# Local attention reads the token-shifted x in place, its tile loop written out

## What is computed

```python
def shift_token(t):                      # second half of the channels from the token before
    t1, t2 = jnp.split(t, 2, axis=-1)
    t2 = jnp.pad(t2, ((0, 0), (1, 0), (0, 0)))[:, :-1]
    return jnp.concatenate([t1, t2], axis=-1)

h = shift_token(x)
q, k, v = jnp.split(h @ wqkv, 3, axis=-1)       # 8 heads of 64
q, k = rotary_xpos(l2norm(q) * qs, l2norm(k) * ksc)
x = x + local_attention(q, k, v) @ wo           # windows of 64, each sees itself and the one before
h = layer_norm(shift_token(x)) * lg + lb
a, g = jnp.split(h @ w1 + b1, 2, axis=-1)
x = x + (a * gelu(g)) @ w2 + b2
```

## Time and profile before

| | us |
|---|---|
| median of 3 runs (1795.16 to 1800.93) | 1795.65 |
| the profiled execution | 1793.86 |
| its span, first to last instruction | 1792.0 |
| first local attention, projection to last add_y | 1199.9 to 1426.7 |
| second | 1489.0 to 1716.4 |
| PE busy | 1565.2 (87%) |
| DVE busy | 1209.4 (67%) |
| ACT busy | 1096.4 (61%) |
| POOL busy | 533.5 (30%) |

### The profile page before, as it was taken

One profiled execution on the slowest core, in us unless ns is written; L12 is line 12 of the kernel. 1 busy time (PEld: TensorE's weight loads), 2 busy tenths in 40 slices (PEclk: granted clock), 3 DMA queues, 4 the chain that ended last, 5 costly groups with the idle time before them and its releaser, 6 DMA issues. The chain is left out here.

```text
span 1792.0 us, 31754 instructions
## 1 busy us (share of the span) xinstructions
PE 1565.2 (87%) x10386; PEld 1060.9 (59%) x10386; DVE 1209.4 (67%) x2313; ACT 1096.4 (61%) x2369; POOL 533.5 (30%) x479
## 2 busy tenths in 40 slices
PE   6999999999769999999888888858888786898875
PEld 4777777777548888888632323325555553656543
DVE  2676676676457777777666766747878646788744
ACT  2555555555258888888546666636776634767641
POOL 1222222232122222222100000027666504666621
PEclk9999999999669999999878988988999998999988
DMA  7000000000012122221000000000000000000000
GB/s 218 1 2 1 0 0 0 0 0 1 0 50 71 70 70 71 75 75 60 0 0 1 1 0 1 1 1 1 1 1 0 0 1 1 1 2 0 0 0 24
DMA packets 18812, 36.05 MB, mean 20 GB/s; under 512 B 5606, under 2 KB 10850, under 8 KB 16546
## 3 DMA queue, kind: packets, MB, share of 16 engines
q1 hardware_dynamic: 18738, 35.08, 5.8%
HBM read 33.90 MB, written 1.18 MB: 20 GB/s over the span
## 5 line engine op out<-in xcount | busy, mean ns | idle before, releaser
L873 DVE TENSOR_TENSOR m_hidp<-m_hid,m_hidp 128x512 fp32r<-128x512 f32 x260 | 182.1, 725 | 81.8 <-ACT m_hidp L832 81.6
L389 ACT ACTIVATE a_prob<-ps,a_negmax 128x512 f32<-128x512 f32 (+3 forms) x256 | 133.8, 525 | 143.8 <-DVE a_negmax L460 143.8
L837 ACT ACTIVATE m_hid<-ps,pre_w 128x512 f32<-128x512 f32 x260 | 176.9, 685 | 51.5 <-PE ps L937 51.4
L937 PE MATMUL ps<-m_xp,m_w1p 128*128 128x512 f32 x780 | 191.9, 396 | 8.1 <-DVE m_xp L865 7.2
L967 PE MATMUL ps<-m_hidp,m_w2p 128*128 128x512 f32 x768 | 189.1, 394 | 0.0
L1140 ACT ACTIVATE c_sb_pT<-ps 128x1024 f32<-128x1024 f32 x128 | 130.3, 1024 | 89.9 <-PE ps L1321 88.6
L1605 ACT ACTIVATE l_sb_prob<-ps,l_sb_negmax,l_sb_rn 128x192 f32<-128x192 f32 (+1 forms) x256 | 123.9, 494 | 92.1 <-DVE l_sb_negmax L1702 92.0
L344 POOL TENSOR_TENSOR a_qk_r<-a_qk_c,a_qk_s 128x512 f32<-128x512 f32 x64 | 81.5, 1273 | 331.0 <-DVE a_qk_s L451 331.0
L1198 DVE TENSOR_REDUCE c_sb_negmax<-ps 128x2 f32<-128x1024 f32 x128 | 153.8, 1220 | 38.7 <-PE ps L1305 38.2
L937 PEld LDWEIGHTS ps<-m_xp,m_w1p 128*128 128x128 f32 x780 | 148.8, 191 | 41.5 <-DVE m_xp L865 7.3
L967 PEld LDWEIGHTS ps<-m_hidp,m_w2p 128*128 128x128 f32 x768 | 144.1, 188 | 33.7
(11 more groups left out here) (227 smaller groups left out, 3360.9 us busy)
## 6 DMA issues: line engine op xcount, KB each, us to landing
m_gate_all<-m_gates_d SPq DMA_DIRECT2D x16, 1024.0 KB, 4.6
pre_w<-w1T SPq DMA_DIRECT2D x14, 258.0 KB, 2.7
pre_w<-w2T SPq DMA_DIRECT2D x14, 256.0 KB, 2.8
pre_wqkv<-wqkv SPq DMA_DIRECT2D x2, 768.0 KB
...
```

The costliest lines, as they stand in the source:

```text
L389: nc.scalar.activation(prob[:, u % 4, 0:width(p)], score_ps(b, p, j)[:, 0:width(p)], ACT.Exp, bias=negmax[:, u:u + 1], accum_out=den[:, b ...
L837: nc.scalar.activation(hid[:, c % 2, f, :], ps[:, f, :], ACT.Gelu, bias=w1[:, k, FF + f:FF + f + 1]).then_inc(gelu_done, 1)
L873: nc.vector.tensor_tensor(hidp[:, c % 2, 1, f, :], hid[:, c % 2, f, :], hidp[:, c % 2, 0, f, :], ALU.subtract).then_inc(low_done, 1)
L937: ins = nc.tensor.matmul(ps[:, f, :], w1p[:, k, a, f * P:(f + 1) * P], xp[:, b, c, :], start=(i == 0), stop=(i == 2))
```

## The change

The turned x is stored shifted. The new `shift_halves` writes channels 0 to 63 into columns 0 to 511 of `xT_full` and channels 64 to 127 into columns 1 to 512, in two ACT copies of 64x512. `Norm` does so at the end of `attention1` (new argument `shifted`), and `gated_mlp` in place of L1971; the phases before keep the plain xT. The tile's columns are then both halves' operand in place: `shifted` on PE is only a slice. `hT`, its semaphore and its 72 copies go. DVE zeroes column 0 of the upper 64 partitions, which POOL did for all 128. `each_tile` writes out all 16 steps, and the steps leave out what would touch a tile past 15. `spread` waits for add_y of the tile before, which it had through project_v. The diff, cut to its core:

```diff
+def shift_halves(nc, keep, src, b, done):
+    full = keep["xT_full"]
+    nc.scalar.activation(full[0:64, b, 0:S], src[0:64, :], ACT.Copy)
+    nc.scalar.activation(full[64:P, b, 1:S + 1], src[64:P, :], ACT.Copy).then_inc(done, 1)
...
 class Norm:
...
     def scalar(self, act):
         for b in range(NB):
             act.wait_ge(self.turn_mm, b + 1)
-            self.nc.scalar.activation(self.keep["xT"][:, b, :], self.ps[:, self.banks[b], :],
-                                      ACT.Copy).then_inc(self.turn_ev, 1)
+            if self.shifted:
+                shift_halves(self.nc, self.keep, self.ps[:, self.banks[b], :], b, self.turn_ev)
+            else:
+                self.nc.scalar.activation(self.keep["xT"][:, b, :], self.ps[:, self.banks[b], :],
+                                          ACT.Copy).then_inc(self.turn_ev, 1)
...
-    norm = Norm(nc, ctx, keep, ps, [0, 1, 2, 3], x_add, [QUADS * (b + 1) for b in range(NB)], "cn_")
+    norm = Norm(nc, ctx, keep, ps, [0, 1, 2, 3], x_add, [QUADS * (b + 1) for b in range(NB)], "cn_", shifted=True)
...
     def each_tile(eng, step):
-        for t in range(TPB):
-            step(t, t)
-        with eng.Fori(1, NB) as b:
-            for t in range(TPB):
-                step(TPB * b + t, t)
+        for n in range(NT):
+            step(n, n % TPB)
...
-        nc.gpsimd.memset(keep["xT_pad"], 0.0).then_inc(inited, 1)
...
     @block.vector
     def _(dve):
-        def shifted(n, t):
-            b = n // TPB % NB
-            wait_past(dve, v_mm, n)
-            full = keep["xT_full"]
-            nc.vector.tensor_copy(hT[0:64, :], full[0:64, bass.ds(b, 1), bass.ds(t * P + 1, P)]
-                                  .rearrange("p a n -> p (a n)")).then_inc(hT_done, 1)
-            nc.vector.tensor_copy(hT[64:P, :], full[64:P, bass.ds(b, 1), bass.ds(t * P, P)]
-                                  .rearrange("p a n -> p (a n)")).then_inc(hT_done, 1)
+        nc.vector.memset(xs[64:P, :, 0:1], 0.0).then_inc(inited, 1)
         dve.wait_ge(inited, 4)
-        shifted(0, 0)
...
-        shifted(1, 1)
...
         def step(n, t):
-            shifted(n + 2, (t + 2) % TPB)
             rowmax(n, t, 0)
             rowmax(n, t, 1)
-            squares(n + 1)
+            if n + 1 < NT:
+                squares(n + 1)
...
     @block.tensor
     def _(pe):
+        def shifted(n, t):
+            return xs[:, n // TPB, t * P:(t + 1) * P]
-        def project_qk(n):
-            pe.wait_ge(hT_done, 2 * (n + 1))
+        def project_qk(n, t):
...
-                ins = nc.tensor.matmul(ps[:, w, :], hT[:, :], wqkv[:, w, :], start=True, stop=True)
+                ins = nc.tensor.matmul(ps[:, w, :], shifted(n, t), wqkv[:, w, :], start=True, stop=True)
...
         def spread(n):
             pe.wait_ge(r_wide, n + 1)
-            pe.wait_ge(v_ev, n + 3)
+            pe.wait_ge(v_ev, min(n + 3, NT))
+            wait_past(pe, y_add, n)
...
-            project_qk(n + 2)
+            if n + 2 < NT:
+                project_qk(n + 2, (t + 2) % TPB)
...
             act.wait_ge(x2_mm, b + 1)
-            nc.scalar.activation(xT[:, b, :], ps[:, 7, :], ACT.Copy).then_inc(x2_ev, 1)
+            shift_halves(nc, keep, ps[:, 7, :], b, x2_ev)
```

More of the change, by code:

```diff
@@ L108, in __init__ @@
                 load(self.m_w2[i][0:r, k, :], io["l_w2"][i, k * P:k * P + r, :])
+def shift_halves(nc, keep, src, b, done):
+    full = keep["xT_full"]
+    nc.scalar.activation(full[0:64, b, 0:S], src[0:64, :], ACT.Copy)
+    nc.scalar.activation(full[64:P, b, 1:S + 1], src[64:P, :], ACT.Copy).then_inc(done, 1)
 class Norm:
[L115 removed]
+    def __init__(self, nc, ctx, keep, ps, banks, ready, counts, prefix, shifted=False):
         def sb(name, shape):
@@ L1498, in each_tile @@
     def each_tile(eng, step):
-        for t in range(TPB):
-            step(t, t)
-        with eng.Fori(1, NB) as b:
-            for t in range(TPB):
-                step(TPB * b + t, t)
-    def first(n):
-        return isinstance(n, int) and n == 0
+        for n in range(NT):
+            step(n, n % TPB)
     @block.gpsimd
@@ L1632, in step @@
             exps(n, t, 1)
-            if not first(n):
+            if n:
                 copy_o(n - 1)
             copy_pT(n, t, 1)
-            copy_qk(n + 2)
+            if n + 2 < NT:
+                copy_qk(n + 2)
             exps(n, t, 2)
             exps(n, t, 3)
-            copy_qT(n + 1, (t + 1) % TPB)
+            if n + 1 < NT:
+                copy_qT(n + 1, (t + 1) % TPB)
             copy_pT(n, t, 3)
-            copy_kT(n + 1, (t + 1) % TPB)
-            squares(n + 2)
-            copy_v(n + 2, (t + 2) % TPB)
+            if n + 1 < NT:
+                copy_kT(n + 1, (t + 1) % TPB)
+            if n + 2 < NT:
+                squares(n + 2)
+            if n + 2 < NT:
+                copy_v(n + 2, (t + 2) % TPB)
         each_tile(act, step)
@@ L1722, in add_y @@
             dve.wait_ge(y_mm, n + 1)
-            xt = x[:, bass.ds(n, 1), :].rearrange("p a d -> p (a d)")
-            nc.vector.tensor_tensor(xt, m_ps[:, 0:D], xt, ALU.add).then_inc(y_add, 1)
-        shifted(1, 1)
+            nc.vector.tensor_tensor(x[:, n, :], m_ps[:, 0:D], x[:, n, :], ALU.add).then_inc(y_add, 1)
         rope_c(0, 0)
@@ L1732, in step @@
         def step(n, t):
-            shifted(n + 2, (t + 2) % TPB)
             rowmax(n, t, 0)
             rowmax(n, t, 1)
-            squares(n + 1)
+            if n + 1 < NT:
+                squares(n + 1)
             copy_pT(n, t, 0)
-            rope_sum(n + 1)
+            if n + 1 < NT:
+                rope_sum(n + 1)
             rowmax(n, t, 2)
             rowmax(n, t, 3)
-            if not first(n):
+            if n:
                 normalise(n - 1)
@@ L1744, in step @@
             reciprocal(n, t)
-            rope_c(n + 2, (t + 2) % TPB)
-            if not first(n):
+            if n + 2 < NT:
+                rope_c(n + 2, (t + 2) % TPB)
+            if n:
                 add_y(n - 1)
@@ L1761, in project_qk, with project_v @@
             for w in range(2):
-                ins = nc.tensor.matmul(ps[:, w, :], hT[:, :], wqkv[:, w, :], start=True, stop=True)
+                ins = nc.tensor.matmul(ps[:, w, :], shifted(n, t), wqkv[:, w, :], start=True, stop=True)
             ins.then_inc(qk_mm, 1)
-        def project_v(n):
-            pe.wait_ge(hT_done, 2 * (n + 1))
+        def project_v(n, t):
             wait_past(pe, y_add, n - 2)
             wait_past(pe, v_ev, n)
-            nc.tensor.matmul(m_ps, hT[:, :], wqkv[:, 2, :], start=True, stop=True).then_inc(v_mm, 1)
+            nc.tensor.matmul(m_ps, shifted(n, t), wqkv[:, 2, :], start=True, stop=True).then_inc(v_mm, 1)
         def turn_qk(n, w):
-            pe.wait_ge(raw_done, n + 2)
+            pe.wait_ge(raw_done, min(n + 2, NT))
             pe.wait_ge(qk_norm if w else rope_add, n + 1)
@@ L1840, in output @@
             ins.then_inc(y_mm, 1)
-        project_qk(0)
-        project_v(0)
-        project_qk(1)
-        project_v(1)
+        project_qk(0, 0)
+        project_v(0, 0)
+        project_qk(1, 1)
+        project_v(1, 1)
         turn_qk(0, 0)
@@ L1858, in step @@
             values(n, t, 0)
-            if not first(n):
+            if n:
                 spread(n - 1)
-            turn_qk(n + 1, 0)
+            if n + 1 < NT:
+                turn_qk(n + 1, 0)
             turn_p(n, t, 2)
-            turn_qk(n + 1, 1)
+            if n + 1 < NT:
+                turn_qk(n + 1, 1)
             turn_p(n, t, 3)
-            if not first(n):
+            if n:
                 output(n - 1)
-            project_v(n + 2)
+            if n + 2 < NT:
+                project_v(n + 2, (t + 2) % TPB)
         each_tile(pe, step)
```

13 lines of the change are left out of this document (5 added, 8 removed).

## The result

The changed kernel takes 1775.0 us (median of 4 runs, 1774.23 to 1779.49) against 1796.09 for the kernel before on the same chip (4 runs, 1795.16 to 1800.93): a ratio of 0.9877, 95% interval 0.9848 to 0.9906. The forecast was 1773.0, with a range from 1764 to 1786. The profiled execution took 1775.55 us, its span 1773.7.

What follows compares the result with a forecast made beforehand. A loop of waits across engines, none full, was taken to pace local attention. Gains of 22.7 (steps) and 3.65 (starts) less 4.7 (added copies) gave 21.65 us: 1772.2 from 1793.86, 1774.0 from 1795.65; forecast 1773, range 1764 to 1786.

Steps and rivals of the forecast that it cites:

- Written-out steps: Local attention, steps the loop had rolled: gains of 0.35 us (t = 2, 3), 0.75 (t = 0), 0.8 (t = 1) each.
- the 0.16 just named: Steps with t = 2, 3: part of hT's 0.71 us left at rope_sum, counted inside the 0.35, not added.
- the cover by project_qk: Steps with t = 2, 3: project_qk on PE holds the first transposes, leaving 0.16 of hT's 0.71 us.
- Step 1: Local attention's n = 1, already written out before the change: claimed to gain 0.5 us.
- Last two steps: n = 14, 15: without work on nonexistent tiles 16 and 17 (spare tiles), 4.6 us a layer gained; bounds 2.0 and 6.5.
- Starts: Starts of both layers' local attention without hT copies: 3.65 us gained, some 2.7 in layer 1, 0.95 in layer 0.
- the slow-clock rival: Layer starts: PE's low clock may last 2.5 us longer at each start; 1778 us, chance 8%.
- The added copies: MLP and attention end: two 64-partition copies cost 0.73 us more than one; 4.7 us lost in all.
- Holding power: Rival, local attention: POOL's power holds DVE's rope_sum, 27 steps lose 0.43 us; 1785 us, chance 5%.
- Covered elsewhere: Rival, local attention: hT's 0.71 us never reach a step's end; about 1785 us, chance 17%.
- Collision gone: Rival: DVE's third negmax product slips ahead of POOL's k_n, some 12 steps gain 0.5 more; 1767 us, chance 12%.
- Instruction supply: Rival: fetching 12 written-out steps a layer costs more than 0.9 us a step; 1801 us at 1.2, chance 4%.

Runs made afterwards that it cites:

- e1: Changed kernel with the tile hT and its DVE copies put back, x stored turned by one copy, tiles still written out; 1781.02 us.
- e2: Kernel before, still rolled and with the work of tiles 16 and 17, but without hT: PE reads stored columns in place; 1788.35 us.
- e4b: Changed kernel with the turned x stored by one copy of 128x512 instead of two of 64 partitions, shift left out; 1772.90 us.
- e5: Changed kernel with the negated row maxima written to PSUM instead of SBUF, so the negmax product has one SBUF input; 1761.71 us.

## Why the prediction held, step by step

**Written-out steps.** Right in kind, each a little small: t = 2, 3 forecast 0.35, measured 0.48; t = 0 0.75 and 0.87; t = 1 0.8 and 0.91. The step that was off is "that includes the 0.16 just named", together with "a written-out step gains about nothing more". The comparison of rolled and written-out steps in one trace holds the loop's price alone, 0.33 (e1), and reading in place brings 0.15 more, also at n = 2 and 3 (12.93 to 12.78). What was misread is "the copy of the transposes already starts at its bound". In e1 that copy is

```profile
1364.01 0.68 DVE L1713 COPY l_sb_probT<-ps 128x512 f32<-128x512 f32 x1
```

4.85 us behind its mask, without a wait for PE; in the changed kernel it starts at +4.75 after 0.63 idle for PE, and k_n ends at +7.69 instead of +7.82. The 0.16 that I had worked out for the cover by project_qk was right and should have been added.

**Step 1.** The 0.5 for n = 1 was wrong: 13.00 to 12.97, and e1 and e2 agree with 13.01 and 12.98.

**Last two steps.** 4.6 against 4.73 and 4.83, but by other items: the spare tiles 3.77, the loop 0.5, hT 0.45, where I had 3.1, 0.35 and 1.15. project_qk, which stood only in the upper bound, is in part on the path.

**Starts.** The step that failed: "product, second projection and k_n move by two such copies and a little, some 2.7 us". The product did: counted from the first projection it starts 2.67 us earlier (5.02 against 7.69). k_n did not follow. In layer 1 it starts 11.49 us behind the first projection, 1.56 earlier than the 13.05 of e1: with the copies gone DVE took the shared access first, POOL's product grew from 2.52 to 3.51, and the clamp behind it from 0.17 to 1.22. Of the 1.56 the clock took more than half in this execution: the turn of k 1.08 instead of e1's 0.63, the first step 11.55 instead of 11.13. That is the slow-clock rival in a small way, 0.9 of its 2.5 us a start in layer 1; in layer 0 the first step was at the lower clock before the change as well (12.27 both times), and of the 0.95 forecast there the 0.45 behind the first projection became 0.06. The other 0.5, that PE no longer waits for hT, did come and went to the second copy at the norm's end: 6.35 before, 6.32 in the changed kernel, 5.71 in e4b, which has one copy and no hT.

**The added copies.** 0.73 a batch: measured 0.74 and 0.75. After batch 2 slack does cover it (14.83 both times from the last scaled copy to the last batch's copy of x). The end of layer 1 cost 2.67 where 2.06 stood; e4b puts 1.70 of it on the copies; 0.43 lie in the MLP's first batch, 10.00 against 9.57, which varies as much without a change, and the other half microsecond I can't place.

**Rivals.** Holding power: refuted by rope_sum's 1.22 under a power of 1.64 in every steady step. Covered elsewhere: refuted by e1, where hT costs 4.4 us in layer 0's steps 1 to 13. Collision gone: did not happen by itself, and e5 shows what it would have brought, 16.88 us in the tail where I gave it 6 (12 steps, 0.5 each): the negmax product was held in 38 places, not in 12. Instruction supply: 0.18 + 0.05 = 0.23 MB more code were fetched, on the queues' 1.20 MB, and no step shows it; t = 2 and 3 are equal, 12.77 to 12.79, from n = 2 to 11.

That the total came out within 0.3 us of the sum in the tail is luck: 2.9 us too little in the steps stood against 1.9 too much at the starts and 0.7 too little for the added copies.
